# Cross attention probabilities turned in four row tiles of 32 queries, one bank per 32 queries of all heads, in a new order of work

## What is computed

```python
x = x + _L0_attn_ref(_layernorm(x), ...)            # and x again inside: 16 heads of 8, no mask in effect
x = x + _L0_xattn_ref(_layernorm(x), ctx, ctx, ...) # 16 heads of 64, rotary, own and 32 earlier keys
x = x + _L0_ffn_ref(_layernorm(x), ...)             # 8 experts, the best one by router, and a shared one
```

```python
scores = jnp.einsum('bhqd,bhkd->bhqk', qh, kh) * DH ** (-0.5)
scores = jnp.where(window_mask, scores, -1e+30)
probs = jax.nn.softmax(scores, axis=-1)
out = jnp.einsum('bhqk,bhkd->bhqd', probs, vh)
```

## Time and profile before

| | |
|---|---|
| median of 3 runs | 795.1 us (792.56 to 796.78) |
| the profiled execution | 793.52 us, of it a span of 790.7 us |
| busy: PE, PEld | 759.4, 631.8 us |
| busy: DVE, ACT, POOL | 536.6, 539.2, 535.4 us |
| granted PE clock, mean | 0.987 of full |
| PE instructions | 10349 matmuls, as many loads |

### The profile page before, as it was taken

One profiled execution on the slowest core, in us unless ns is written; L12 is line 12 of the kernel. 1 busy time (PEld: TensorE's weight loads), 2 busy tenths in 40 slices (PEclk: granted clock), 3 DMA queues, 4 the chain that ended last, 5 costly groups with the idle time before them and its releaser, 6 DMA issues.

```text
span 790.7 us, 28613 instructions
## 1 busy us (share of the span) xinstructions
PE 759.4 (96%) x10349; PEld 631.8 (80%) x10349; DVE 536.6 (68%) x1350; ACT 539.2 (68%) x1900; POOL 535.4 (68%) x864
## 2 busy tenths in 40 slices
PE   7999999999999999999999999999899999999894
PEld 4778878888888888888888888888679778777563
DVE  3466767777777777777777777777866686665553
ACT  1367767777777777777777777777667667666352
POOL 3366777777777777777777777777565666576434
PEclk8999999999999999999999999999999999999998
DMA  6013212222222222222222222223043132133130
GB/s 232 12 56 124 80 61 82 88 91 93 92 93 73 73 73 73 72 73 73 73 73 73 73 73 72 73 73 128 9 129 125 48 101 72 40 104 123 55 101 12
DMA packets 56791, 64.06 MB, mean 81 GB/s; under 512 B 4014, under 2 KB 52916, under 8 KB 56656
## 3 DMA queue, kind: packets, MB, share of 16 engines
q1 hardware_dynamic: 52928, 54.06, 20.9%
q0 software_dynamic: 3008, 6.57, 2.4%
q10 hardware_dynamic: 720, 1.63, 0.5%
HBM read 17.80 MB, written 45.35 MB: 80 GB/s over the span
## 4 chain that ended last, share of the span: by engine, by line
PE 91%; DVE 3%; issue 2%; DMA 1%; ACT 1%; POOL 1%; SPq 0%; POOLq 0%; DVEq 0%; ACTq 0%
PE P L327 8%; PE P L272 8%; PE P L307 7%; PE P L292 7%; PE P L316 7%; PE P L338 7%; PE P L282 7%; PE P L397 5%; PE P L224 4%; PE P L207 4%; PE P L356 4%; PE P L239 4%; PE P L247 2%; PE P L364 2%; PE P L410 1%
## 5 line engine op out<-in xcount | busy, mean ns | idle before, releaser
L799 ACT ACTIVATE PX<-P,mx 128x128 f32<-128x128 f32 x512 | 182.1, 394 | 61.0 <-DVE mx L569 61.0
L966 POOL TENSOR_TENSOR PX<-PX,mx 128x512 f32<-128x512 f32 x128 | 133.0, 1041 | 62.0 <-DVE mx L574 62.0
L569 DVE TENSOR_REDUCE mx<-P 128x4 f32<-128x512 f32 x128 | 82.0, 679 | 119.3 <-PE P L307 119.3
L799 ACT ACTIVATION_READ_ACCUMULATOR PX<-P,mx 128x1 f32 x512 | 119.9, 234 | 0.0
L763 ACT ACTIVATE PS<-P 128x512 f32<-128x512 f32 x128 | 66.1, 602 | 32.0 <-PE P L228 32.0
L999 POOL DMA_INDIRECT out<-yst,xrow x46 | 46.0, 1000 | 54.6 <-DVE yst L673 42.5
L508 DVE TENSOR_REDUCE nmf<-P 128x4 f32<-128x512 f32 x128 | 79.5, 683 | 5.1 <-PE P L207 2.2
L961 POOL TENSOR_TENSOR rq<-rq,tq 128x1024 f32<-128x1024 f32 x32 | 75.7, 2365 | 8.8 <-DVE tq L533 7.8
L808 ACT ACTIVATE PT<-P 128x512 f32<-128x512 f32 x128 | 77.7, 607 | 3.5 <-PE P L316 0.8
L956 POOL TENSOR_TENSOR rk<-rk,tk 128x1024 f32<-128x1024 f32 x32 | 75.5, 2359 | 0.0
L272 PE MATMUL P<-wvT,cxT 128*128 128x512 f32 x128 | 70.4, 633 | 3.0 <-DVE tk L533 3.0
(11 more groups left out here) (144 smaller groups left out, 1757.4 us busy)
## 6 DMA issues: line engine op xcount, KB each, us to landing
z_xs<-c SPq DMA_DIRECT2D x34, 1088.0 KB, 5.3
xrow<-z_xs SPq DMA_DIRECT2D x46, 136.0 KB, 2.1
ew<-in_ew SPq DMA_DIRECT2D x9, 384.0 KB, 6.4
x<-in_x SPq DMA_DIRECT2D x32, 64.0 KB, 1.8
cxT<-in_ctxT SPq DMA_DIRECT2D x31, 64.0 KB, 1.7
out<-yst,xrow POOLq DMA_INDIRECT x46, 2.3
wk<-in_wk SPq DMA_DIRECT2D x1, 512.0 KB, 4.4
wvT<-in_wvT SPq DMA_DIRECT2D x1, 512.0 KB, 7.0
```

The lines of the kernel that those rows point to most:

```text
L569: dve.tensor_reduce(mx[b % 3][:, 0, r, :], v3(bank(f"ds{r}")), AX.X, ALU.max, negate=True).then_inc(S["v_dm"][r], 1)
L799: t = act.activation(PX[(4 * b + r) % 6][:, c, :], p[:, c * 128:c * 128 + 128], ACT.Exp, bias=m[:, 0, r, c:c + 1], scale=1.0, accum_out=m[ ...
L966: pool.tensor_tensor(X[:, :, :], X[:, :, :], mx[b % 3][:, 2, r, :].rearrange("p (h a) -> p h a", a=1).to_broadcast([128, 4, 128]), ALU.mul ...
```

## The change

- `d_t(b)` turns all 16 heads in one place. For each group r and head c, four transposes take 32 queries each (partitions 32a to 32a + 31) and put keys x 32 queries into bank a at columns 128r + 32c. So there are 64 transposes, each in a row tile a, with a moving identity of 32 x 32. A bank then holds 32 queries of all 16 heads. It waits for each group's `p_pn` ahead of that group, and raises one semaphore `t_dt` at the end.
- `d_pt(b, a)` copies bank a to `PT[b % 2][:, :, 32a:32a+32]`; `PT` is two whole arrays of 16 heads. `d_pv` waits for all four copies. `PX` has 7 groups (`NPX`), `xab` 6 buffers for 8, `xhT` 2 for 3.
- The banks, the `WARM` counts and the orders of all five engines are new. In PE's order `d_t` stands behind `b_ln` and ahead of `r_q`; the cross attention after it follows one period earlier in the loop's count (`d_pv` s - 6 for s - 7, and so on).

```diff
+NPX = 7
-BANK = dict(a=1, cnt=5, dn=0, dpv0=1, dpv1=0, ds0=3, ds1=6, ds2=2, ds3=5, dt0=1, dt1=5, dt2=0, dt3=0, et=2, gu=2,
-            kE=1, kO=7, ln=7, nmt=4, oT=1, po=0, pos=7, qE=3, qO=0, qkv=4, rt=5, s0=3, s1=2, s2=5, s3=6, st0=7, st1=6,
-            st2=4, st3=3, v0=4, v1=7, wo=4, x1=5, xg0=4, xg1=1, xg2=7, xg3=1, xgt0=1, xgt1=2, xgt2=3, xr0=6, xr1=3,
+BANK = dict(a=0, cnt=1, dn=2, dpv0=6, dpv1=4, ds0=0, ds1=7, ds2=3, ds3=1, dt0=5, dt1=7, dt2=3, dt3=1, et=3, gu=1,
+            kE=4, kO=5, ln=2, nmt=0, oT=4, po=5, pos=2, qE=2, qO=4, qkv=6, rt=6, s0=0, s1=7, s2=6, s3=2, st0=7, st1=0,
+            st2=2, st3=3, v0=4, v1=5, wo=6, x1=1, xg0=4, xg1=7, xg2=0, xg3=4, xgt0=1, xgt1=2, xgt2=3, xr0=5, xr1=3,
...
-WARM = {('a', 0): 36, ('nmt', 0): 41, ('st0', 0): 9, ('po', 0): 33, ('oT', 0): 13, ('qE', 0): 9, ('st0', 1): 9,
-        ('ds0', 0): 22, ('oT', 1): 28, ('st0', 2): 9}
+WARM = {('a', 0): 36, ('qkv', 0): 8, ('nmt', 0): 14, ('st0', 0): 9, ('po', 0): 33, ('oT', 0): 13, ('qE', 0): 10,
+        ('st0', 1): 10, ('ds0', 0): 30, ('oT', 1): 28, ('st0', 2): 10}
...
-            def d_t(b, r):
-                p = take(f"dt{r}", b, (S["s_pt"][r], b + 1))
-                pe.wait_ge(S["p_pn"][r], b + 1)
-                for c in range(4):
-                    t = pe.transpose(p[:, c * 128:c * 128 + 128], PX[(4 * b + r) % 6][:, c, :], ident[:, :])
-                t.then_inc(S["t_dt"][r], 1)
+            def d_t(b):
+                p = [take(f"dt{a}", b, (S["s_pt"][a], b + 1)) for a in range(4)]
+                for r in range(4):
+                    pe.wait_ge(S["p_pn"][r], b + 1)
+                    for c in range(4):
+                        for a in range(4):
+                            t = pe.transpose(p[a][:, 128 * r + 32 * c:128 * r + 32 * c + 32],
+                                             PX[(4 * b + r) % NPX][32 * a:32 * a + 32, c, :],
+                                             ident[32 * a:32 * a + 32, 32 * a:32 * a + 32])
+                t.then_inc(S["t_dt"], 1)
...
             def d_pv(b, k):
...
-                for r in (2 * k, 2 * k + 1):
-                    pe.wait_ge(S["s_pt"][r], b + 1)
-                    for i in range(2):
-                        for u in range(2):
-                            q = 2 * (r % 2) + i
-                            t = pe.matmul(p[64 * u:64 * u + 64, 128 * q:128 * q + 128], V[b % 3][:, 4 * r + 2 * i + u, :],
-                                          PT[(4 * b + r) % 6][:, 2 * i + u, :], start=True, stop=True)
+                for a in range(4):
+                    pe.wait_ge(S["s_pt"][a], b + 1)
+                for q in range(4):
+                    for u in range(2):
+                        h = 8 * k + 2 * q + u
+                        t = pe.matmul(p[64 * u:64 * u + 64, 128 * q:128 * q + 128], V[b % 3][:, h, :],
+                                      PT[b % 2][:, h, :], start=True, stop=True)
...
+                batch(c_v, s - 4, 1)
...
+                batch(r_k, s - 4, 0)
+                batch(e_tr, s - 7)
...
+                batch(a_qkv, s - 3)
+                batch(b_ln, s - 5)
+                batch(d_t, s - 6)
+                batch(r_q, s - 5, 0)
+                batch(r_q, s - 5, 1)
...
+                batch(b_nm, s - 4)
+                batch(f_up, s - 7)
...
+                batch(b_st, s - 4)
+                batch(d_pv, s - 6, 1)
+                batch(d_pv, s - 6, 0)
+                batch(d_s, s - 5)
+                batch(b_pv, s - 4)
...
+                batch(f_pos, s - 7)
+                batch(d_wo, s - 6)
...
+                batch(b_oT, s - 4)
+                batch(f_dn, s - 7)
...
+                batch(r_k, s - 3, 1)
+                batch(a_tr, s - 2)
+                batch(b_cn, s - 4)
...
+                batch(c_v, s - 3, 0)
+                batch(b_x1, s - 4)
+                batch(b_s, s - 3)
```

More of the change, by code:

```diff
@@ L92, in build @@
         arow = ring("arow", 2, [128, 128])
-        xab = ring("xab", 8, [128, 128])
+        xab = ring("xab", 6, [128, 128])
         aT = ring("aT", 2, [128, 128])
@@ L409, in x_dn @@
                 pe.wait_ge(S["s_xh"], j + 1)
-                pe.matmul(p[:, 0:128], xhT[j % 3][:, 0, :], ewf[:, bass.ds(at[j] + 512, 128)], start=True,
+                pe.matmul(p[:, 0:128], xhT[j % 2][:, 0, :], ewf[:, bass.ds(at[j] + 512, 128)], start=True,
                           stop=False)
-                pe.matmul(p[:, 0:128], xhT[j % 3][:, 1, :], ewf[:, bass.ds(at[j] + 640, 128)], start=False,
+                pe.matmul(p[:, 0:128], xhT[j % 2][:, 1, :], ewf[:, bass.ds(at[j] + 640, 128)], start=False,
@@ L413, in x_dn @@
                           stop=True).then_inc(S["t_xy"], 1)
             for s in range(PERIODS):
[L416 to L426, removed]
@@ L455, in _ @@
-                batch(c_v, s - 4, 0)
-                tile(x_tr, s - 32, 3)
-                batch(b_ln, s - 5)
-                batch(d_t, s - 6, 1)
-                batch(d_t, s - 6, 2)
+                tile(x_tr, s - 32, 2)
+                tile(x_dn, s - 33, 2)
+                tile(x_hT, s - 33, 3)
+                tile(x_up, s - 32, 1)
+                tile(x_tr, s - 32, 3)
+                tile(x_dn, s - 33, 3)
+                batch(r_k, s - 4, 0)
+                batch(e_tr, s - 7)
+                tile(x_hT, s - 32, 0)
@@ L525, in b_x1 @@
                 dve.wait_ge(S["p_xab"], b + 1)
-                dve.tensor_tensor(xab[b % 8][:, :], bank("x1")[:, 0:128], xab[b % 8][:, :], ALU.add).then_inc(S["v_x1"], 1)
+                dve.tensor_tensor(xab[b % 6][:, :], bank("x1")[:, 0:128], xab[b % 6][:, :], ALU.add).then_inc(S["v_x1"], 1)
                 dve.wait_ge(S["v_x1"], b + 1)
@@ L579, in d_y @@
                     dve.wait_ge(S["v_fy"], b - 3)
-                dve.tensor_tensor(x2[b % 4][:, :], bank("wo")[:, 0:128], xab[b % 8][:, :], ALU.add).then_inc(S["v_y"], 1)
+                dve.tensor_tensor(x2[b % 4][:, :], bank("wo")[:, 0:128], xab[b % 6][:, :], ALU.add).then_inc(S["v_y"], 1)
                 dve.wait_ge(S["v_y"], b + 1)
@@ L700, in _ @@
+                batch(b_x1, s - 5)
+                batch(d_ri, s - 6, 2)
+                batch(b_max, s - 4, 2)
+                batch(b_max, s - 4, 3)
+                batch(b_max, s - 4, 1)
+                tile(x_gate, s - 32, 0)
                 tile(x_y, s - 33, 2)
-                batch(b_x1, s - 5)
-                batch(a_v, s - 4)
-                batch(d_ri, s - 6, 2)
-                batch(d_ri, s - 6, 0)
+                batch(b_max, s - 4, 0)
+                tile(x_gate, s - 32, 1)
@@ L705, in _ @@
+                tile(x_y, s - 33, 3)
                 batch(r_k1, s - 4)
-                tile(x_y, s - 33, 3)
-                tile(x_gate, s - 32, 0)
-                batch(b_max, s - 4, 2)
-                batch(b_max, s - 4, 0)
-                batch(b_max, s - 4, 3)
+                batch(a_km, s - 3)
+                tile(x_gate, s - 32, 2)
+                batch(a_v, s - 3)
+                batch(r_q1, s - 5)
+                batch(r_q3, s - 5)
+                batch(f_route, s - 7)
+                batch(f_gate, s - 7)
@@ L711, in _ @@
+                batch(a_stats, s - 1)
+                tile(x_y, s - 32, 0)
+                batch(d_max, s - 5, 0)
+                batch(d_max, s - 5, 2)
+                batch(d_max, s - 5, 3)
+                batch(f_pos, s - 7)
+                batch(d_max, s - 5, 1)
             for j in range(TILE0[1], NT + 4):
```

183 lines of the change are left out of this document (75 added, 108 removed).

## The result

The changed kernel takes 809.4 us (807.1 to 813.2) where the kernel before took 793.8 us beside it (792.3 to 796.8): a ratio of 1.0196, 95% interval 1.0144 to 1.0248. The forecast was 781 us in a range of 770 to 809, and slower was given 0.23. The profiled execution of the changed kernel took 813.2 us with a span of 811.2, 20.5 us above the span before. It is the slowest of the four, and the one before is among the fastest of its own, so the traces show some 4 us more than the 15.6 between the medians.

The account below looks back on a forecast made before the run. PE's instructions were taken to bound the 20.31 us period; 30 batches at 0.44 us less (13.2) and ends minus 1 gave 14 us off the profiled 793.5, 779.5, or 781 as median; range 770 to 809.

Parts of the forecast that it names:

- The turning itself: Turning of the probabilities on PE: 16 rounds at 57 ns, 0.92 us a batch, where it cost 1.76 us.
- 0.40 us of tiling: PE entering and leaving row tiles once more per batch, around the turning: 0.40 us, between 0.25 and 0.55.
- The gain of 0.44 us a batch: PE's turning plus tiling changes, 1.32 us against 1.76: 0.44 us less a batch (0.25 to 0.6), period 19.87 us.
- The order: All four probability pieces must be normalised before the turning ends; last piece ready with half a microsecond to spare, no cost.
- the loop of 19.25 us: Loop through exponentials, last normalisation, turning, and `r_q` to the end of `d_s`: 19.25 us against a 19.87 period, not binding.
- the four copies: ACT's copies of the turned banks, now together, 2.1 to 2.5 us behind the turning: cost nothing, margin 0.1 to 0.5.
- Ends: Start, warming products, table of tiles and drain outside the ordinary periods: minus 1 us together.
- The stall at the table: PE's 1.49 us wait for DVE's table of tiles, more work now queued behind it: plus 2 us, between 0 and 4.
- The start: First `c_v` no longer waits 2.99 us for DVE's first table product, its bank being free: minus 2 us, 0 to minus 3.
- Issue: PE gets 96 more instructions a batch; 64 pairs at 14.4 ns take the same 0.92 us, a slower feed not excluded.
- swapped banks and earlier stages: Work moved on DVE, ACT, POOL and SP, engines said to have 5 of 20 us left; no cost counted.
- rival B: Load or feed sets the turning's round at 107 to 121 ns, slower from 85 ns: 805 to 812 us, chance 0.18.

## Why the prediction was wrong

- *The turning itself, 16 rounds of 57 ns and 0.40 us of tiling: 1.32 us.* Measured 1.11 + 0.09 + 0.11 = 1.31. The sum was right by luck, by two errors that cancel: a round is 69 ns, not 57, and the changes cost 0.20, not 0.40. The loads are shown at 137 ns (141 forecast from the turned tile), far from the 187 of loads with products. The rule of the Trainium skill (TensorE: Matmul & The Clock Gate, "LDWEIGHTS (loading the stationary operand)", 107 ns for 128 columns whatever the rows) would have made the rounds alone 1.71 us, an estimate, and is not borne out for turned row tiles: 69 ns a round. Nor is that page's 25 ns from start to start ("Wait — 56ns, not 53.3ns?"): 17.3 ns a pair over 64 pairs.
- *The gain of 0.44 us a batch.* The row tiles bring exactly that (20.46 to 20.02). The term that the sum lacked is the order's own cost, 0.15 us: `b_s` enters row tiles directly behind `b_x1`, whose two passes take 0.39 us to the next step (270.86 to 271.25) where they took 0.22 (275.03 to 275.25 in the kernel before). So 0.29 a batch, 7 us where 10.6 was forecast by batch 25.
- *The order: the loop of 19.25 us does not bind; the four copies cost nothing.* Right: no wait for another engine in an ordinary period, and the copies that write with gaps take what the ones in a row took:

```profile
276.39 2.06 ACT L811 ACTIVATE PT<-P 128x512 f32<-128x512 f32 x4 [0.70 <-PE P L320]
278.42 0.28 ACT L759 ACTIVATE nmT<-P 128x128 bf16<-128x128 bf16 x1
```

- *Ends.* The stall at the table was to grow by 2: it is 3.14 us at 556.03 where it was 1.49. The start was to win 2: `c_v(0)` has no wait (9.34), but `c_v(1)` waits 3.08 us for the same table product at 14.62, and the first `d_s` starts at 42.7 for 43.0. Among the kernels of this study that start lies anywhere from 38.7 to 43.0, so no such term can be told from one execution.
- *The step that failed: "Issue", with "swapped banks and earlier stages ... move work on engines that have 5 of 20 us left".* The feed was asked about once, for the ordinary period, and handed to rival B as a uniform pace. There it is no trouble: 17.3 ns a pair over 64 pairs, under B's 85 ns a round. It fails only in five batches, where PE runs register loads and POOL makes scatters, both of which were moved by the new order and costed at nothing, because their engines and their queue were not full. (In the last five batches of the kernel before no two scatters in a row stand beside a step of 64 pairs.) What a moved step collides with was not asked. B's time (805 to 812) holds the result; its mechanism is not what happened, and the range ended at 809 with no case in it that hits a few batches hard and the others not at all.
- *Where the price comes from.* From 8.0 us ahead at batch 27 to 20.5 behind: a collapse of 1.8 to 2.5 us in the turning of each of five batches, then the lowered clock behind it, then `d_s`.

Shown by runs: the sends' scatters are needed (without them, or with POOL busy otherwise, it is gone); the register loads and the sums on them are both needed; a step with many pairs is needed (16 wide ones are not hit, 64 narrow ones are, and three `d_s` of 64 pairs less hard); moving three loads, or holding the scatters back, ends it; the old pace is back about half a microsecond after the last scatter. A busy POOL, the bytes sent and late blocks of instructions are not the cause. Not shown: by what path PE's instructions are held up. The 39 to 46 matmuls before the first idle, in every slow turning of four kernels, look like a stock that is used up while only six to twelve instructions arrive every 0.73 us, but why three moved loads restore it and one or two do not is open.

## What to carry to other kernels

A change that multiplies the instructions of a step makes that step sensitive to how instructions reach its engine. Look in every stage of the kernel, not in the ordinary period alone, for what will stand beside it: scatters made on POOL, register loads on its own engine. When a stage slows down with idles that end in "issue", try first to move the register loads some steps ahead and to hold the scatters back to a step with few instructions; and compare with the same repair on the kernel before, since it helped that one by 0.7% too.

## What was not expected of the hardware

- Four row tiles turn 32 queries x 128 keys each in 69 ns a round, fp32, 64 pairs at 17.3 ns, and a turned tile's load is shown at 137 ns where a load with products is shown at 187.
- PE's feed can fall to three to six matmuls with their loads every 0.73 us, with no semaphore waited for, while POOL makes scatters of 128 rows back to back (1.0 to 1.1 us each). Three register loads moved some steps earlier end it (1.11 us a turning, where moving one of them leaves 3.58 with scatters at the same places).
- A few microseconds of such idling are paid twice: PE, busy 2.88 of 4 us, was granted 0.55 and 0.59 in the following four, and 16 passes took 2.97 us for 1.89.
- Register loads on PE cost 8 us in 46 tiles even where nothing collapses (782.5 against 774.2 us, single runs, wrong experts in both), and sums on a register nothing (773.6).
